# The inverse deviation of every LayerNorm as an exponential of a logarithm, in the tail of a vision tower

## The reference

```python
def _layernorm(x, axis=-1, eps=1e-05):
    m = jnp.mean(x, axis=axis, keepdims=True)
    v = jnp.var(x, axis=axis, keepdims=True)
    return (x - m) / jnp.sqrt(v + eps)
...
h = h + attention(_layernorm(h))      # 8 heads of 8, a window of 32 tokens to each side
h = h + ffn(_layernorm(h))            # 64 experts of 64x64, the best 6 per token
...
# the end of ffn(x):
    h = x + proj
    mu = jnp.mean(h, axis=-1, keepdims=True)
    var = jnp.mean(jnp.square(h - mu), axis=-1, keepdims=True)
    return (h - mu) * jax.lax.rsqrt(var + LN_EPS) * ln_g + ln_b
```

## Time and profile before

| | |
|---|---|
| median of 3 runs | 1065.15 us (1063.59 to 1070.08) |
| the profiled execution's own time | 1065.44 us |
| its span | 1063.6 us |
| TensorE busy | 962.6 us (91%) |
| VectorE busy | 613.7 us (58%) |
| ScalarE busy | 397.5 us (37%) |
| GpSimd busy | 152.4 us (14%) |
| chain that ended last | PE 71%, DVE 13%, ACT 4% |

### The profile page before, as it was taken

The page is one execution under the profiler, slowest core; times in us unless marked ns, Lnnn a source line. Parts: engine busy times, 40 slices in busy tenths (PEclk is TensorE's granted clock), DMA queues, the critical chain, the costliest instruction groups (busy, mean ns, idle before and its releaser), DMA issues.

```text
span 1063.6 us, 36547 instructions
## 1 busy us (share of the span) xinstructions
PE 962.6 (91%) x17004; PEld 619.0 (58%) x17004; DVE 613.7 (58%) x771; ACT 397.5 (37%) x524; POOL 152.4 (14%) x160
## 2 busy tenths in 40 slices
PE   4899999989989998999899999989888799678896
PEld 3576666656756633566567657657415587633343
DVE  2267457726844322477358548733244577768997
ACT  1333323233223387232233323223695567421200
POOL 6000000000000000000000000020000575325432
PEclk9999999999999999999999999999999899869999
DMA  6220131022011400410220031020011000000000
GB/s 197 97 79 3 40 109 30 4 94 80 3 65 49 143 5 12 121 50 3 95 80 3 15 122 40 3 95 18 2 24 47 1 2 2 1 1 1 1 7 16
DMA packets 25931, 46.78 MB, mean 44 GB/s; under 512 B 9962, under 2 KB 11013, under 8 KB 25138
## 3 DMA queue, kind: packets, MB, share of 16 engines
q1 hardware_dynamic: 24131, 42.47, 12.9%
q0 software_dynamic: 1456, 1.63, 0.6%
q10 hardware_dynamic: 192, 0.33, 0.1%
HBM read 30.25 MB, written 10.89 MB: 39 GB/s over the span
## 4 chain that ended last, share of the span: by engine, by line
PE 71%; DVE 13%; issue 5%; ACT 4%; DMA 2%; POOL 2%; SPq 1%; DVEq 0%; POOLq 0%
PE PSALL L1363 22%; PE PSALL L1331 8%; PE PSALL L1222 5%; PE PSALL L1354 5%; PE PSALL L1306 4%; PE PSALL L1236 4%; PE PSALL L550 3%; DVE WORK L1577 3%; PE PSALL L449 3%; DVE WORK L1064 2%; PE PSALL L1421 2%; DVE WORK L1596 2%; PE PSALL L536 2%; PE PSALL L1199 2%; PE PSALL L1350 2%
## 5 line engine op out<-in xcount | busy, mean ns | idle before, releaser
L1596 DVE STREAM_TRANSPOSE WORK<-PSALL 128x1024 f32<-128x1024 f32 x128 | 152.5, 1230 | 251.4 <-PE PSALL L1331 251.4
L1363 PEld LDWEIGHTS PSALL<-EW,WORK 128*64 128x64 f32 x4096 | 221.8, 138 | 72.8 <-issue 48.3
L1363 PE MATMUL PSALL<-EW,WORK 128*64 128x128 f32 x4096 | 247.6, 276 | 14.0 <-DVE WORK L1596 13.8
L1496 ACT ACTIVATE X<-PSALL,TABLES 128x1024 f32<-128x1024 f32 x128 | 141.8, 1114 | 306.5 <-PE PSALL L1363 306.5
L1577 DVE STREAM_TRANSPOSE WORK<-PSALL 128x1024 f32<-128x1024 f32 x84 | 104.3, 1242 | 32.7 <-PE PSALL L1222 30.9
L347 POOL DMA_DIRECT2D WORK<-MIXED x32 | 17.6, 550 | 666.0 <-ACT MIXED L1487 555.6
L1478 ACT COPY SPEC<-PSALL 128x400 f32<-128x400 f32 x64 | 54.0, 850 | 139.1 <-PE PSALL L1236 132.8
L1236 PEld LDWEIGHTS PSALL<-TABLES,WORK 128*64 128x64 f32 x2000 | 67.5, 139 | 47.4 <-DVE WORK L1577 31.4
L1064 DVE TENSOR_TENSOR WORK<-PSALL,X 128x910 f32<-128x910 f32 (+1 forms) x80 | 79.4, 1018 | 16.0 <-PE PSALL L536 14.4
L1236 PE MATMUL PSALL<-TABLES,WORK 128*64 128x64 f32 x2000 | 81.1, 228 | 7.5 <-DVE WORK L1577 3.9
L1530 ACT ACTIVATE WORK<-PSALL,B 128x1024 f32<-128x1024 f32 x64 | 68.2, 1114 | 8.3 <-PE PSALL L1421 7.3
(11 more groups left out here) (165 smaller groups left out, 1150.4 us busy)
## 6 DMA issues: line engine op xcount, KB each, us to landing
SW<-in_spec_w SPq DMA_DIRECT2D x160, 80.0 KB, 2.7
spec_scr<-MIXED SPq DMA_DIRECT2D x24, 400.0 KB, 3.2
SPEC<-spec_scr SPq DMA_DIRECT2D x32, 200.0 KB
WORK<-spec_scr SPq DMA_DIRECT2D x16, 200.0 KB
WORK<-in_coords_w SPq DMA_DIRECT2D x2, 1024.0 KB, 4.8
XC<-in_coords_c SPq DMA_DIRECT2D x2, 1024.0 KB, 7.1
WORK<-MIXED SPq DMA_DIRECT2D x40, 40.0 KB
WORK<-MIXED POOLq DMA_DIRECT2D x32, 40.0 KB
```

The costliest lines, as they stand in the source:

```text
L1363: m = pe.matmul(PS[2 * p + z][64 * j:64 * j + 64, 2 * b * GRID:(2 * b + 2) * GRID], G[:, n % 2, b, h:h + 2, :, t].rearrange("p q o -> p (q ...
L1496: nc.scalar.activation(X[:, n].rearrange("p b (z d) c w -> p d z b (c w)", z=2)[:, p, :, :, 2 * t * GRID:2 * (t + 1) * GRID], PSALL[:, 2 * ...
L1596: nc.vector.transpose(G[:, n % 2, 2 * x + y].rearrange("p h o v -> p o h v"), PSALL[:, 4 + 2 * x:6 + 2 * x, :].rearrange("p k (h o v) -> p ...
```

## The change

The Sqrt on ScalarE and the reciprocal on VectorE give way to two activations on ScalarE: the logarithm of the variance, and the exponential of minus one half of it, which writes `st[:, 3]` itself. The second waits for the first on a new semaphore, `logarithms_ready`. VectorE loses its 13 reciprocals. In the norm ahead of the experts it used to wait for the deviation at the reciprocal, one step ahead of the products; it now waits at the first product.

```diff
             def deviation(n, k):
+
                 a = slice(k * LB, (k + 1) * LB) if n < 2 else LASTS[k]
                 act.wait_ge(var_ready, n * LK + k + 1)
-                nc.scalar.activation(st[:, 2, a], st[:, 1, a], ACT.Sqrt).then_inc(dev_ready, 1)
+                logs[0] += 1
+                nc.scalar.activation(st[:, 2, a], st[:, 1, a], ACT.Ln).then_inc(log_ready, 1)
+                act.wait_ge(log_ready, logs[0])
+                nc.scalar.activation(st[:, 3, a], st[:, 2, a], ACT.Exp, scale=-0.5).then_inc(dev_ready, 1)
...
             def deviations(n, k):
                 a = slice(k * LB, (k + 1) * LB)
                 dve.wait_ge(dev_ready, n * LK + k + 1)
-                link(nc.vector.reciprocal(st[:, 3, a], st[:, 2, a]))
                 return a
...
-                        if 0 < k <= LK and step == 0:
-                            dve.wait_ge(dev_ready, LK + k)
-                            nc.vector.reciprocal(st[:, 3, past], st[:, 2, past]).then_inc(inverse_ready, 1)
                         if 0 < k <= LK and step in (1, 2):
                             at = slice((k - 1) * LB + (step - 1) * BC, (k - 1) * LB + step * BC)
-                            dve.wait_ge(inverse_ready, k)
+                            dve.wait_ge(dev_ready, LK + k)
...
                 def last_scale(k, src, done):
                     a = LASTS[k]
                     dve.wait_ge(dev_ready, 2 * LK + k + 1)
-                    link(nc.vector.reciprocal(st[:, 3, a], st[:, 2, a]))
```

More of the change, by code:

```diff
@@ L312, in vit_kernel @@
         dve_step = sem("dve_step")
+        log_ready = sem("logarithms_ready")
         var_ready, dev_ready = sem("variance_ready"), sem("deviation_ready")
@@ L591, in feature_rows @@
                 nc.scalar.copy(YT[0:rows, c * CT:(c + 1) * CT], PS[c % 2][0:rows, 0:CT]).then_inc(yt_ready, 1)
+            logs = [0]
             def deviation(n, k):
```

## The result

| | before | after |
|---|---|---|
| median | 1066.41 us (1063.59 to 1070.08, 4 runs) | 1085.59 us (1075.13 to 1090.38, 4 runs) |
| the profiled execution's own time | 1065.44 us | 1090.38 us |
| its span | 1063.6 us | 1088.6 us |
| granted TensorE clock, mean over its span | 0.983 | 0.960 |

The ratio is 1.0173 (95%: 1.0136 to 1.021): slower, as forecast, but by twice as much, and outside the range. Executions of one kernel, the one before included, differ by some microseconds with the granted clock.

What follows compares the result with a forecast made beforehand. TensorE bound the queries' stretch, short steps of four engines waiting in turn 920 to 950 us, VectorE and TensorE the rest. Terms summed to 9.6 us over the median 1065.15, giving 1074.8; range 1069.5 to 1080.5.

Steps and rivals of the forecast that it cites:

- The direct terms: Call-by-call costs of the added loads and activations in the tail's three norms, summing to 9.6 us.
- Blocks 0 to 2 of the first norm: Six loads and six activations after the last Gelu, hidden before ScalarE's next task with 0.4 us to spare: 0.
- Block 3 of the second norm: Two loads where the call paid none; exponential 2.93 us behind the old Sqrt, delaying TensorE's next transpose: +2.0 us.
- Block 2: Second norm: exponential ends 1.73 us later, delaying VectorE's product and the work queued behind it: +1.1 us, at least 0.5.
- parts 1 to 4: Last norm: VectorE's products wait longer for the exponential, +0.7, +1.1, +1.1 and, at the chain's end, +1.9 us.
- part 0: Last norm: product can start 0.36 us later, about half passed on: +0.2 us, bounds 0 and 0.36.
- first norm, block 3: +1.3: Logarithm, load and exponential delay the query bias, so TensorE's next projection starts 1.3 us later; bounds 0.7 and 2.1.
- a lower clock as a rival: Half clock lasting into the expert stage, or a second stretch where attention fills its pipeline: 1077.3, up to 1079; chance 0.13.
- the terms left: The direct terms without the projections' 1.3 us, which idle products cover: 8.3 us.
- Theory 1: From the experiments: the projections' 1.3 us wait brings a clock fall costing what the sum lacks; direct terms hold.
- The rival of dearer loads: Each of about ten added loads on the path costs its length again in draining: 12.8 us more, 1088; chance 0.03.
- one table for both: Logarithm and exponential share a table, loads fall from nine to one: about 1064 us; chance 0.04.

Runs made afterwards that it cites:

- after_both_filled: Changed kernel plus idle TensorE products at chunk 5 of the projections and behind the scores of the attention's first four images; 1073.95 us, ratio 1.0064.
- the two filled kernels: after_both_filled and logs_second_last_filled, at 1073.95 and 1073.64 us.
- the control: Kernel before plus idle TensorE products at chunk 5 of the projections and behind the scores of the attention's first four images; 1064.74 us, ratio 0.9985.
- after_filled: Changed kernel plus two idle TensorE products behind the transposes of chunk 5 in the projections, where TensorE waited; 1076.78 us, ratio 1.0103.
- logs_second_last: Kernel before with logarithm and exponential in the second and last norms only, root and reciprocal kept in the first; 1077.82 us, ratio 1.0112.
- logs_second_last_filled: logs_second_last plus one idle TensorE product behind the scores of each of the attention's first four images; 1073.64 us, ratio 1.0066.
- logs_first: Kernel before with logarithm and exponential in the first norm only, Sqrt and reciprocal in the other two; 1075.96 us, ratio 1.0067.
- before_delayed: Kernel before plus three 0.64 us ScalarE copies behind the fourth Sqrt of the first norm, no table load added; 1066.9 us, ratio 1.0059.

## Why the prediction missed

**The direct terms were right.** Blocks 0 to 2 of the first norm are covered. On ScalarE, after the last Gelu:

```profile
804.66 0.21 ACT L603 ACTIVATE st<-st 65x8 f32<-65x8 f32 x1
806.69 0.64 ACT L592 COPY X<-PSALL 64x260 f32<-64x260 f32 x2 [1.83 <-PE PSALL L370]
```

Six loads are over at 804.87, and ScalarE then waits 1.83 us for TensorE, whose opening transposes start at 806.26 (forecast near 806.8). The spare time is more than the 0.4 us that were forecast because the last Gelu ended 1.9 us earlier here than in the profile before; in after_both_filled it is 0.32. TensorE's wait ahead of its first projection is 0.23 us in all three, so the cover held.

Block 3 of the second norm, whose exponential was forecast 2.93 us behind the old root, at a cost of 2.0 in TensorE's steps:

```profile
953.89 0.21 ACT L601 ACTIVATE st<-st 65x8 f32<-65x8 f32 x1
954.12 1.28 ACT L603 ACT_TABLE_LOAD   x1
955.41 0.21 ACT L603 ACTIVATE st<-st 65x8 f32<-65x8 f32 x1
955.53 0.61 ACT L656 CAST SW<-SW 64x520 bf16<-64x520 f32 x1
955.65 1.29 DVE L1026 TENSOR_TENSOR X<-X,st 65x512 f32<-65x512 f32 x2 [3.72 <-ACT st L603]
```

The logarithm to the end of the exponential is 1.73 us, as worked out from the earlier trace rows, and the stage lost 2.1. Block 2 cost 1.0, read in the two filled kernels as the distance from its first activation to the first part of the expert scores, 7.4 us against 6.4 (forecast 1.1).

The last norm's products on VectorE:

```profile
1042.06 0.69 DVE L1057 TENSOR_TENSOR X<-XC,st 65x512 f32<-65x512 f32 x1 [0.78 <-ACT st L603]
...
1055.77 0.69 DVE L1057 TENSOR_TENSOR X<-XC,st 65x512 f32<-65x512 f32 x1 [0.78 <-ACT st L603]
...
1072.81 0.69 DVE L1057 TENSOR_TENSOR X<-XC,st 65x512 f32<-65x512 f32 x1 [1.19 <-ACT st L603]
...
1077.99 0.42 DVE L1057 TENSOR_TENSOR X<-XC,st 65x256 f32<-65x256 f32 x1 [1.19 <-ACT st L603]
...
1085.55 0.42 DVE L1057 TENSOR_TENSOR X<-X,st 65x256 f32<-65x256 f32 x1 [2.49 <-ACT st L603]
```

The fourth of these products in the kernel before:

```profile
1055.01 0.42 DVE L1055 TENSOR_TENSOR X<-XC,st 65x256 f32<-65x256 f32 x1
```

The distances from one product to the next, less those before (the first three and the last in the earlier trace rows), are 0.6, 1.0, 1.1 and 1.9 us for parts 1 to 4; part 0 lost 0.3 from the start of the stage. Forecast were 0.7, 1.1, 1.1, 1.9 and 0.2. VectorE had little spare time there (99.49 of 113 us busy), and the waits add up.

The end, on ScalarE:

```profile
1082.43 1.28 ACT L601 ACT_TABLE_LOAD   x1
...
1083.72 0.20 ACT L601 ACTIVATE st<-st 65x4 f32<-65x4 f32 x1
1083.95 1.28 ACT L603 ACT_TABLE_LOAD   x1
1085.24 0.20 ACT L603 ACTIVATE st<-st 65x4 f32<-65x4 f32 x1
```

**The step that failed is the clock.** The term "first norm, block 3: +1.3" priced a wait by its length, with bounds of 0.7 and 2.1, as if the clock of 1.00 held behind it. The prediction had a lower clock as a rival, at a chance of 0.13: "Five microseconds at 1.2 GHz where 2.4 was granted cost at most 2.5: 1077.3, up to 1079", deciding at the start of the expert stage or where the attention fills its pipeline. It took the length of the half clock from the length of the slip. The runs showed something else. The fall came at the wait of that term itself, 146 us ahead of the first spread gate value of the expert stage. It lasted some 41 us, and 10 more followed at 900, behind a TensorE wait of 1.63 us (from 896.39) at the second norm's first pair of loads. A longer half stretch was among the prediction's own signs of being wrong. In these two stages the changed kernel had about 18.7 us of half clock in the projections (817.7 to 836.4) and 32 in the attention (836.4 to 859 and 900 to 910), against 0 and 7 before. That is 44 us more. At most half of that, 22, could be lost; the table of stages shows 15.9. The term itself was right as a wait (1.27 us), and wrong as a price: together with what followed it, it cost 9.5 us in its own stage.

The trace of before held a hint that the prediction did not use: the 7 us at 0.52 from 834 to 841, 6 us behind the first scores. The prediction read the clock of 810 to 828 (1.00) and of 920 to 950 (0.54), and took the first for a property of the stretch. The hint would have put the question of what a new wait does to the clock there; it did not tell the length of the fall.

**The sum tested by itself.** With TensorE kept busy at both places, the change costs 9.2 us where 8.3 was forecast for the terms left, and 1073.95 us is in the predicted range. That the two agree so well is in part luck. In the two profiled executions the four stages are 11.1 us longer than the control's: 0.4 more in the projections than forecast, 1.3 more in the attention (the short fall) and 1.0 in the last norm, where another fall at 1062.7 catches TensorE's last products (1.91 and 1.14 us, against 1.27 and 0.69 in the changed kernel). The tail started 1.2 us earlier in this execution than in the control's, which hides as much. Theory 1 holds for the projections (after_filled). At the first images of the attention idle products take the half clock away too (logs_second_last against logs_second_last_filled), but the waits there are those of the kernel before: what that place adds is not shown to be a price of the change. The rival of dearer loads falls: in every row above a load's user starts 0.01 to 0.02 us behind it, and the loads between a logarithm and its exponential start 0.02 to 0.03 us behind the logarithm. The Trainium skill ("ScalarE: Activation LUTs", section "What ACT_TABLE_LOAD costs") adds about 1.38 us of draining to a load; these rows do not bear it out. The rival "one table for both" was right about the direction, and short on the size: a gain of 1 us was forecast (1064), 3.6 were measured (1061.47 against 1065.08). The Trainium skill (the same page, "Table sets: the hidden batching unit") has both functions in one set; by these runs that is so once the set is loaded by name (3 loads), and not by itself (28).

**What stays open.** Why the fall follows the wait in some executions and not in others (5 of 12 with the delayed root, at least 7 of 12 in logs_first) is not settled, nor why TensorE, busy for most of the time after it, got its clock back only at 859. The traces hold one hint. The two profiled executions with the fall in the projections, those of the changed kernel and of logs_first, both also have the fall of 3.4 us near 800, ahead of the opening transposes. That of before_delayed has the wait but neither fall, and that of the control has a fall at 802 but no wait, and keeps its clock. So the earlier fall may be a condition of the later one; with one trace per kernel this is not shown. The trace of after_filled has neither fall, so that its idle products prevent the later one rests on its five times and the six of after_both_filled. What moves the tail's start is open too: the first projection starts between 805.0 and 808.5 us in the twelve profiled executions, though nothing ahead of the tail was changed. That is enough to hide the control's gain of 1.3 us (attention 2.4 shorter, projections 1.1 longer) in its median.

## What to carry to other kernels

A wait of a microsecond on TensorE, where it paces a stage, can have two prices: itself, and what the granted clock does after it. Before adding a small wait to TensorE's path, look for half-clock stretches nearby in the kernel as it is and price the rest of the stage at half clock as a rival of its own. Before putting two functions in a row on ScalarE, read the built order for loads between them; if one set holds both, load that set by name: the same change turned from 1.0173 into 0.9972.

## What the runs showed that was not expected

TensorE, after a wait of 1.27 us, ran at 1.2 GHz for about 41 us while busy 27.85 of the 31 us from 828 to 859. Idle products of some 1.5 us (1.08 and 0.38) in the place of the wait kept the clock at 1.00 through the projections and took 8.8 us off the median (1085.59 to 1076.78, not side by side, but each beside the kernel before). The same kernel on the same chip differs by up to 16 us between executions when such a wait is in it (logs_first: 1063.24 to 1079.08), so a single timing of it says little without its granted clock.
